# Expert layers without a barrier between them: weight pieces loaded as their rooms come free, small inputs loaded once

## The chip, the cores and the metric

One core of one Trainium2 chip. The time is device microseconds of one execution of the whole program on that core; a kernel's time is the median of its runs.

## What is computed

A network of four graph layers over 3125 nodes with 128 features and 100000 edges: a gated graph unit, two convolutions, a relational layer with 8 edge types, and a mixture of experts. Only the last one is touched:

```python
deg = jnp.clip(segment_sum(ones, dst), 1.0)[:, None]
h = x @ W_in + b_in                                   # 3125 x 256
for l in range(3):
    agg = segment_sum(h[src], dst) / deg
    logits = concatenate([h, agg], -1) @ router_W[l] + router_b[l]      # 8 experts
    gates = softmax of the top 2 of logits, 0 elsewhere
    weak = relu(einsum('nh,ehf->nef', agg, weak_W[l]) + weak_b[l])      # 4 experts
    sh = relu(einsum('nh,ehf->nef', agg, strong_W1[l]) + strong_b1[l])  # 4 experts, 512 wide
    strong = einsum('nef,efh->neh', sh, strong_W2[l]) + strong_b2[l]
    moe = einsum('ne,neh->nh', gates, concatenate([weak, strong], 1))
    h = h + sigmoid(h @ conf_W[l] + conf_b[l]) * moe
return h @ W_out + b_out
```

## The kernel before, in words

Edges are turned once into a dense matrix of counts (`A`, the tile `counts`), so that every segment sum is a matrix product on TensorE. The expert layer's code is `block_experts`. Its **input stage** parks the features `xn` in DRAM (`sp_inputs`), normalizes them (the norm runs over groups of tiles, in turns of VectorE and ScalarE) and makes `m_h`, 25 tiles of 128 nodes by 256. A barrier ends it. Then come **three layers**, each closed by a barrier of all engines. `dve_layer`, `act_layer`, `pe_layer` and `sp_layer` write down, engine by engine, the work of one layer; within an engine the order is that of the code, and between engines semaphores order it.

A layer goes like this.
- VectorE reduces `m_h` to its largest magnitude (L1738 over all of `m_h` in the first layer, L1740 over the seven chunk maxima that L1905 left in the others), TensorE spreads it (L2002, L2004), and VectorE makes a power-of-two scale of it; L1749 is the last step.
- ScalarE casts the scaled `m_h` to half precision in five pieces (L1921), VectorE writes the remainders (L1754); both halves feed the **edge sums** on TensorE (L2018), 100 matmuls for a chunk of up to 512 nodes.
- The weights come as ten pieces of 512 KB (four first matrices `w1`, four second matrices `w2`, two pairs of weak matrices `ww`) in the order of `ORDER`. Piece k is loaded as f32 into room k + 1 and split into two halves of f16 in room k, by ScalarE (L1928) and VectorE (L1772) in turn; the tenth piece is loaded into a spare part of `x_nodes`. Four pieces are split before the first chunk, the others inside it.
- Then seven chunks: the mean of the edge sums with the inverse degrees `m_invd` (L1783), the router (L2042), hidden products (L2057), strong products (L2076), weak products (L2093), and VectorE adds each expert to `m_h` (L1865, L1881). The last chunk has 309 nodes. In it the hidden blocks of expert e come in two halves, the second one after the strong products of expert e - 1.

The loads of a layer are issued from two queues. SyncE's: the ten pieces (L1720, L1724), then `m_invd` for each chunk (L1731), each of the latter after the mean of the chunk before. ScalarE's, at the very start of `act_layer` and so ahead of the casts in its program: the router's weights and biases (`m_rw`, `m_rb`, L1912 to L1915), the strong experts' hidden biases `m_b` (L1916, 2048 single elements) and the output biases `m_bias` (L1917, L1918, each repeated over 128 partitions).

Of the kernel before, what the change touches and what calls it, by code (L numbers as in the profile page):

```python
# [25 lines left out]
P = 128  # L26
# [23 lines left out]
def build_program(nc, x, src, dst, et, g_w, g_ih, g_hh, g_bih, g_bhh, c_w0, c_b0, c_w1, c_b1,  # L50
# [1503 lines left out]
    mrw_in, mb1_in, mbb_in, inv_in = sem("mrw_in"), sem("mb1_in"), sem("mbb_in"), sem("inv_in")  # L1554
# [10 lines left out]
    def block_experts(part):  # L1565
        SL = 2 * BANK
        NPC = 2 * NSG + NWK // 2
        NSH = 6
        NPR = NWK * H // BANK
        with ExitStack() as c:  # L1570
            h2 = sbuf(c, "m_h", [P, NT, H], F32)
            bcast = sbuf(c, "m_bias", [P, NE * H], F32)
            agg = sbuf(c, "m_agg", [P, KB, BANK], F32)
            agg16 = sbuf(c, "m_agg16", [P, 2, KB, BANK], F16)
            hT = sbuf(c, "m_hT", [P, KB, BANK], F32)
            rw = sbuf(c, "m_rw", [P, 2 * KB, NE + 1], F32)
            rb = sbuf(c, "m_rb", [P, NE + 1], F32)
# [6 lines left out]
            wmax, wsc, winv, wwork = (sbuf(c, f"m_wmax{i}", [P, NM], F32) for i in range(4))  # L1584

            with ExitStack() as c0:
# [6 lines left out]
                def pool_inputs():  # L1593
                    pool.iota(prio[:], pattern=[[-1, NE]], base=NE, channel_multiplier=0,
                              allow_small_or_imprecise_dtypes=True).then_inc(prio_made, 1)

                def sp_inputs():
                    sp.dma_start(xpark, xn[:].rearrange("p i f -> p (i f)")).then_inc(parked, 16)
                    sp.wait_ge(parked, 16)
# [62 lines left out]
            with ExitStack() as c0:  # L1662
                h16 = sbuf(c0, "m_h16", [P, 2, NT, H], F16)
                wroom = sbuf(c0, "m_weights", [P, NPC, SL], F32)
                b1 = sbuf(c0, "m_b1", [P, NSG * FB], F32)
# [47 lines left out]

                def sp_layer(l):
                    for k, (n_, e) in enumerate(ORDER):
                        room = loaded_piece(k)
                        if n_ == "ww":
                            r3 = room.rearrange("p (k f) -> p k f", k=KB)
                            for x_ in range(2):
                                sp.dma_start(r3[:, :, x_ * H:(x_ + 1) * H],  # L1720
                                             m_ww[l, 2 * e + x_].rearrange("(k p) h -> p k h", p=P)).then_inc(piece_in[k], 16)
                        else:
                            w_, nb = (m_w1, KB) if n_ == "w1" else (m_w2, FB)
                            sp.dma_start(room.rearrange("p (k f) -> p k f", k=nb),  # L1724
                                         w_[l, e].rearrange("(k p) f -> p k f", p=P)).then_inc(piece_in[k], 16)
                    for ci in range(NCH):
                        n = l * NCH + ci
                        c_, cw = CH[ci]
                        if n:
                            sp.wait_ge(e_mean, KB * n)  # L1730
                        sp.dma_start(invd[:, 0:cw], bass.AP(invd_row.tensor, c_, [[0, P], [1, cw]])).then_inc(inv_in, 16)  # L1731

                def dve_layer(l):
                    w_inv = {n_: scale_of(l, n_, winv) for n_ in ("w1", "w2", "ww")}
                    if l == 0:
                        vec.memset(rw[:, KB:2 * KB, NE:NE + 1], 0.0).then_inc(steps.handle, steps.up())
                        mark["rw_cleared"] = steps.n
# [17 lines left out]
                    vec.wait_ge(mb1_in, 16 * (l + 1))  # L1755
# [8 lines left out]
                    vec.tensor_scalar(b1s[:], b1[:], ks[:, 1:2], None, ALU.mult).then_inc(steps.handle, steps.up())  # L1764
# [23 lines left out]
                    def route(ci):  # L1788
# [3 lines left out]
                        vec.wait_ge(mrw_in, 64 * (l + 1))  # L1792
# [3 lines left out]
                                          rb[0:R_, None, :].to_broadcast([R_, n_, NE + 1]), ALU.add).then_inc(e_logits, 1)  # L1796
# [112 lines left out]
                def act_layer(l):  # L1909
                    if l == 0:  # L1910
                        act.wait_ge(steps.handle, mark["rw_cleared"])
                    act.dma_start(rw[:, :, 0:NE], m_rw[l].rearrange("(k p) e -> p k e", p=P)).then_inc(mrw_in, 16)  # L1912
                    act.dma_start(rw[:, 0:KB, NE:NE + 1], m_cw[l].rearrange("(k p) e -> p k e", p=P), allow_slow_non_contiguous=True).then_inc(mrw_in, 16)
                    act.dma_start(rb[:, 0:NE], bass.AP(m_rb.tensor, m_rb.offset + l * NE, [[0, P], [1, NE]])).then_inc(mrw_in, 16)
                    act.dma_start(rb[:, NE:NE + 1], bass.AP(m_cb.tensor, m_cb.offset + l, [[0, P], [1, 1]])).then_inc(mrw_in, 16)  # L1915
                    act.dma_start(b1[:], m_b1[l].rearrange("e (k p) -> p (e k)", p=P), allow_slow_non_contiguous=True).then_inc(mb1_in, 16)  # L1916
                    act.dma_start(bcast[:, 0:NWK * H], bass.AP(m_wb.tensor, m_wb.offset + l * NWK * H, [[0, P], [1, NWK * H]])).then_inc(mbb_in, 16)  # L1917
                    act.dma_start(bcast[:, NWK * H:NE * H], bass.AP(m_b2.tensor, m_b2.offset + l * NSG * H, [[0, P], [1, NSG * H]])).then_inc(mbb_in, 16)  # L1918
# [80 lines left out]
                def pe_layer(l):  # L1999
# [33 lines left out]
                    def route(ci):  # L2033
# [3 lines left out]
                        pe.wait_ge(mrw_in, 64 * (l + 1))  # L2037
                        for i, k in tiles_of(CH[ci]):
                            r_ = rows_of(i)
                            for kk in range(2 * KB):  # L2040
                                lhs = (hT if kk < KB else agg)[:, kk % KB, k * P:k * P + r_]
                                m = pe.matmul(bank[2][0:r_, k * (NE + 1):(k + 1) * (NE + 1)], lhs, rw[:, kk, :],  # L2042
# [802 lines left out]
```

## Time and profile before

| | us |
|---|---|
| median of 3 runs | 3355.61 (3353.94 to 3356.59) |
| profiled execution, its own time | 3354.32 |
| span of the profile | 3352.3 |
| TensorE matmul busy in the span | 2990.9 (89%) |
| VectorE busy | 2184.1 (65%) |
| ScalarE busy | 897.6 (27%) |

The profiled execution takes 2.0 us more than its span; the sum of the prediction is made against its time. The three expert layers are the last 1,590 us of the span but for some 33 us of output. A row of a timeline below gives: start, duration, engine, line, operation, out<-in, count, and in brackets the idle time before with what ended it. A row with SPq or ACTq is a DMA issue on the queue of SyncE or ScalarE, and its duration is the time that the issue took there, not the transfer.

### The profile page before, as it was taken

What the parts mean: (1) busy time and instruction counts of PE and PEld (TensorE: products, weight loads), DVE (VectorE), ACT (ScalarE), POOL (GpSimd) and SP (SyncE); (2) the same over time, 40 slices, a digit from 0 to 9 for tenths busy, and PEclk for the clock granted to TensorE, in tenths of its full rate; (3) what the DMA queues carried; (4) which work ended last, traced back from release to release, by engine and by line L of the source; (5) the groups of instructions that cost most, each with busy time, mean ns of one, the idle gap of its engine ahead of it and who ended that gap; (6) DMA issues with size and microseconds to landing.
All of it is one profiled execution on the core that took longest, in us unless ns stands there. A gap on an engine that the chain in (4) does not pass through costs nothing. (4 is left out here: it accounts for less than half of the span.)

```text
span 3352.3 us, 47544 instructions
## 1 busy us (share of the span) xinstructions
PE 2990.9 (89%) x18761; PEld 1803.0 (54%) x18761; DVE 2184.1 (65%) x3982; ACT 897.6 (27%) x1667; POOL 16.6 (0%) x22
## 2 busy tenths in 40 slices
PE   3777889999797999999959999988999998999997
PEld 2555555555343444444535655664656564566565
DVE  7999555554426667666666666675666675666666
ACT  3887322121212000000023222323222233222222
POOL 1000000000000000000000000000000000000000
PEclk8898999999898999999979999998999998999999
DMA  4544456563003555554330000002000002000001
GB/s 103 155 140 145 134 184 205 189 209 125 21 1 116 172 154 171 171 155 130 88 104 4 6 3 4 3 3 80 3 4 4 5 1 82 3 4 3 4 3 40
DMA packets 310670, 262.56 MB, mean 78 GB/s; under 512 B 32735, under 2 KB 289377, under 8 KB 308142
## 3 DMA queue, kind: packets, MB, share of 16 engines
q1 hardware_dynamic: 295406, 252.86, 24.7%
q10 hardware_dynamic: 14624, 5.76, 0.7%
q8 instruction: 153, 2.51, 0.3%
q0 software_dynamic: 416, 0.85, 0.1%
q14 instruction: 71, 0.58, 0.1%
HBM read 171.03 MB, written 88.41 MB: 77 GB/s over the span
## 5 line engine op out<-in xcount | busy, mean ns | idle before, releaser
L1437 PE MATMUL psum<-r_wd,r_h 128*128 128x512 fp8e4 (+1 forms) x2600 | 567.9, 374 | 13.3 <-ACT r_h L226 12.7
L2057 PE MATMUL psum<-m_agg,m_weights 128*128 128x512 f16 (+2 forms) x2016 | 423.1, 362 | 34.2 <-ACT m_agg L1964 34.2
L2018 PE MATMUL psum<-counts,m_h 128*128 128x512 fp8e4 (+2 forms) x2100 | 416.0, 354 | 29.0 <-DVE m_h L1754 29.0
L2076 PE MATMUL psum<-m_weights,x_nodes 128*128 128x256 f16 (+1 forms) x3600 | 413.0, 273 | 17.6 <-DVE m_wtmp L1862 15.9
L1437 PEld LDWEIGHTS psum<-r_wd,r_h 128*128 128x128 f16 x2600 | 240.0, 96 | 306.1 <-issue 16.8
L2076 PEld LDWEIGHTS psum<-m_weights,x_nodes 128*128 128x128 f16 (+1 forms) x3600 | 350.3, 98 | 75.1 <-DVE m_wtmp L1862 22.6
L2057 PEld LDWEIGHTS psum<-m_agg,m_weights 128*128 128x128 f16 x2016 | 197.3, 101 | 243.1 <-issue 50.1
L2018 PEld LDWEIGHTS psum<-counts,m_h 128*128 128x128 f16 x2100 | 206.2, 98 | 225.3 <-issue 35.5
L1976 ACT ACTIVATE m_hT<-m_hT,m_g 128x256 f32<-128x256 f32 x300 | 135.4, 500 | 599.5 <-DVE m_hT L1876 599.5
L1964 ACT ACTIVATE m_agg<-psum,x_nodes 128x512 f32<-128x512 f32 (+2 forms) x336 | 236.4, 717 | 145.6 <-PE psum L2057 116.2
L627 PE MATMUL psum<-oh_c,oh_s 128*128 128x150 f16 x1566 | 159.4, 244 | 84.2 <-ACT counts L653 63.5
L1862 DVE SCALAR_TENSOR_TENSOR m_wtmp<-psum,x_nodes,m_bias 128x256 f32<-128x256 f32 (+1 forms) x300 | 144.9, 483 | 120.3 <-PE psum L2076 116.8
L1876 DVE SCALAR_TENSOR_TENSOR m_hT<-psum,x_nodes,m_bias 128x512 f32<-128x512 f32 (+1 forms) x150 | 111.9, 750 | 169.7 <-PE psum L2093 169.7
L1853 DVE TENSOR_TENSOR x_nodes<-m_agg,x_nodes 128x512 f16<-128x512 f32 (+2 forms) x336 | 209.7, 624 | 11.6
L2093 PE MATMUL psum<-m_weights,m_agg 128*128 128x512 f16 x900 | 206.5, 379 | 0.0
L810 DVE TENSOR_TENSOR sym_blocks<-sym_blocks,psum 128x1024 uint16<-128x1024 uint16 (+1 forms) x169 | 110.3, 664 | 115.7 <-PE psum L791 115.3
L1452 ACT ACTIVATE r_ags<-psum 128x512 f32<-128x512 f32 (+1 forms) x52 | 26.9, 569 | 581.3 <-PE psum L1437 581.3
L627 PEld LDWEIGHTS psum<-oh_c,oh_s 128*128 128x128 f16 x1566 | 114.3, 102 | 126.7 <-issue 94.0
L652 ACT ACTIVATE strip<-psum 128x600 uint16<-128x600 f32 x239 | 162.0, 678 | 35.9 <-PE psum L627 32.9
L922 PE MATMUL psum<-counts,g_h 128*128 128x512 fp8e4 (+2 forms) x700 | 156.8, 358 | 8.0 <-PEq L104 5.0
L922 PE MATMUL psum<-counts,g_h16b 128*128 128x512 fp8e4 (+2 forms) x700 | 151.0, 352 | 5.5 <-DVE g_h16b L1074 5.5
L1865 DVE SCALAR_TENSOR_TENSOR m_h<-m_wtmp,m_g,m_h 128x256 f32<-128x256 f32 (+1 forms) x300 | 145.3, 484 | 10.7
(284 smaller groups left out, 3363.6 us busy)
## 6 DMA issues: line engine op xcount, KB each, us to landing
r_wd<-packed_sym SPq DMA_DIRECT2D x120, 640.0 KB, 4.2
packed_counts<-strip SPq DMA_DIRECT2D x21, 1800.0 KB, 7.7
sym_blocks<-packed_counts SPq DMA_DIRECT2D x88, 384.0 KB, 4.5
packed_sym<-sym_blocks SPq DMA_DIRECT2D x84, 384.0 KB, 3.3
w_stage<-in_L_gnn_strong_W SPq DMA_DIRECT2D x12, 1024.0 KB, 6.4
m_weights<-in_L_gnn_strong_W SPq DMA_DIRECT2D x21, 512.0 KB, 9.3
w_stage<-in_L_gnn_weak_W SPq DMA_DIRECT2D x3, 1024.0 KB, 6.1
m_weights<-in_L_gnn_weak_W SPq DMA_DIRECT2D x12, 256.0 KB, 9.7
```

The costliest lines, as they stand in the source:

```text
L627: m = pe.matmul(psum[:, unit_at(u, w):unit_at(u, w) + UC], oh_s[q][:, k, :, v], oh_c[q][:, k, :, v], start=True, stop=True)
L652: act.activation(typed_home, typed, ACT.Copy, scale=0.5).then_inc(kept_a, 1)
L922: m = pe.matmul(bank[bk][:, 0:cw], h16[l % 2][:, part, i, :], A[:, i, c_:c_ + cw], start=(i == 0 and part == 0), stop=(i == NT - 1 and par ...
L1437: m = pe.matmul(bank[pair[b]][:, 0:2 * cw], h16[:, part, p0 + i, :], f_[:, 2 * b:2 * b + 2, :], start=(p0 + i == 0 and part == 0), stop=(p ...
L1853: vec.tensor_tensor(s_[:, BANK:BANK + cw], wide32, s_[:, 0:cw], ALU.subtract).then_inc(s_split, 1)
L1862: vec.scalar_tensor_tensor(tmp[k % 2][0:r_, :], bank[6 + k % 2][0:r_, 0:H], k_strong[0:r_], bcast[0:r_, ge * H:(ge + 1) * H], ALU.mult, AL ...
L1865: vec.scalar_tensor_tensor(h2[0:r_, i, :], tmp[k % 2][0:r_, :], gates[ci % 2][0:r_, k, ge:ge + 1], h2[0:r_, i, :], ALU.mult, ALU.add).then ...
L1964: act.activation(agg[:, hh % 2, 0:cw], bank[4 + hh % 2][:, 0:cw], ACT.Relu, bias=b1s[:, e * FB + f:e * FB + f + 1], scale=k_hidden).then_i ...
L2018: m = pe.matmul(bank[kb][:, 0:cw], h16[:, part, i, kb * P:(kb + 1) * P], A[:, i, c_:c_ + cw], start=(i == 0 and part == 0), stop=(i == NT ...
L2057: m = pe.matmul(bank[4 + hh % 2][:, 0:cw], w_[:, i, kb, f * P:(f + 1) * P], agg16[:, j, kb, 0:cw], start=(x_ == 0), stop=(x_ == len(todo) ...
L2076: m = pe.matmul(bank[b_][0:r_, 0:H], s_[:, pa[0] * BANK + k * P:pa[0] * BANK + k * P + r_], w_[:, pa[1], f, :], start=(f == 0 and pa == PA ...
L2093: m = pe.matmul(bank[2 + pr % 2][0:r_, :], agg16[:, pa[0], kb, k * P:k * P + r_], w_[:, pa[1], kb, :], start=(y_ == 0), stop=(y_ == len(to ...
```

## The change

- The barrier at the end of each layer goes; one stays behind the last layer.
- `sp_layer` waits, from the second layer on, before it loads piece k, until the layer before has finished with the room that piece k goes into (`room_used`).
- The small inputs `m_rw`, `m_rb` and `m_b` get room for all three layers and are loaded once, in the input stage, by SyncE. The output biases `m_bias` keep one room; SyncE loads them in the input stage for the first layer, and for a later one after the last strong expert of the layer before was added.
- ScalarE issues no DMA in the layers. The clearing of a column of `m_rw` goes from VectorE to GpSimd.

```diff
@@ block_experts @@
-            rw = sbuf(c, "m_rw", [P, 2 * KB, NE + 1], F32)
-            rb = sbuf(c, "m_rb", [P, NE + 1], F32)
+            b1 = sbuf(c, "m_b1", [P, NLAY, NSG * FB], F32)
+            rw = sbuf(c, "m_rw", [P, NLAY, 2 * KB, NE + 1], F32)
+            rb = sbuf(c, "m_rb", [P, NLAY, NE + 1], F32)
...
+            def load_biases(l):
+                sp.dma_start(bcast[:, 0:NWK * H], bass.AP(m_wb.tensor, m_wb.offset + l * NWK * H, [[0, P], [1, NWK * H]])).then_inc(mbb_in, 16)
+                sp.dma_start(bcast[:, NWK * H:NE * H], bass.AP(m_b2.tensor, m_b2.offset + l * NSG * H, [[0, P], [1, NSG * H]])).then_inc(mbb_in, 16)
...
                 def sp_inputs():
                     sp.dma_start(xpark, xn[:].rearrange("p i f -> p (i f)")).then_inc(parked, 16)
+                    sp.wait_ge(prio_made, 2)
+                    for l in range(NLAY):
+                        sp.dma_start(rw[:, l, :, 0:NE], m_rw[l].rearrange("(k p) e -> p k e", p=P)).then_inc(mrw_in, 16)
+                        sp.dma_start(rw[:, l, 0:KB, NE:NE + 1], m_cw[l].rearrange("(k p) e -> p k e", p=P), allow_slow_non_contiguous=True).then_inc(mrw_in, 16)
+                        sp.dma_start(rb[:, l, 0:NE], bass.AP(m_rb.tensor, m_rb.offset + l * NE, [[0, P], [1, NE]])).then_inc(mrw_in, 16)
+                        sp.dma_start(rb[:, l, NE:NE + 1], bass.AP(m_cb.tensor, m_cb.offset + l, [[0, P], [1, 1]])).then_inc(mrw_in, 16)
+                        sp.dma_start(b1[:, l], m_b1[l].rearrange("e (k p) -> p (e k)", p=P), allow_slow_non_contiguous=True).then_inc(mrw_in, 16)
+                    load_biases(0)
                     sp.wait_ge(parked, 16)
...
+                def room_used(l, k):
+
+                    if k + 1 == NPC:
+                        sp.wait_ge(s_mixed, NSG * NT * (l + 1))
+                        return
+                    n_, e = ORDER[k + 1]
+                    if n_ == "w1":
+                        sp.wait_ge(s_hidden, hidden_at(l, NCH - 1, e, FB - 1) + 1)
+                    elif n_ == "w2":
+                        sp.wait_ge(s_mixed, mixed_at(l, NCH - 1, e, len(tiles_of(CH[NCH - 1])) - 1) + 1)
+                    else:
+                        sp.wait_ge(k_mixed, NPR * NT * (l + 1))
+
                 def sp_layer(l):
                     for k, (n_, e) in enumerate(ORDER):
                         room = loaded_piece(k)
+                        if l:
+                            room_used(l - 1, k)
...
+                    if l:
+                        sp.wait_ge(s_added, NSG * NT * l)
+                        load_biases(l)
                     for ci in range(NCH):
...
                 def act_layer(l):
-                    if l == 0:
-                        act.wait_ge(steps.handle, mark["rw_cleared"])
-                    act.dma_start(rw[:, :, 0:NE], m_rw[l].rearrange("(k p) e -> p k e", p=P)).then_inc(mrw_in, 16)
...
-                    act.dma_start(bcast[:, NWK * H:NE * H], bass.AP(m_b2.tensor, m_b2.offset + l * NSG * H, [[0, P], [1, NSG * H]])).then_inc(mbb_in, 16)
                     act.wait_ge(steps.handle, mark["h_scale", l])
...
                     pe_layer(l)
                     sp_layer(l)
-                    barrier()
+                barrier()
```

How the issues move. First ScalarE before the change, at the start of the second layer: the last six reliefs of the layer before, then the seven issues, the five casts, and the first splits.

```order
L1964 ACTIVATE m_agg<-psum,x_nodes 128x309 x6
L1912 DMA m_rw<-in_L_gnn_router_W 128x4x8
L1913 DMA m_rw<-in_L_gnn_conf_W 128x2x1
L1914 DMA m_rb<-in_L_gnn_router_b 128x8
L1915 DMA m_rb<-in_L_gnn_conf_b 128x1
L1916 DMA m_b_127<-in_L_gnn_strong_b 128x16x1
L1917 DMA m_bias<-in_L_gnn_weak_b 128x1024
L1918 DMA m_bias<-in_L_gnn_strong_b 128x1024
L1921 ACTIVATE m_h_125<-m_h,m_sc 128x1280 x5
L1928 ACTIVATE m_weights<-m_weights,m_wmax_114 128x1024 x4
```

All seven DMA rows are gone from ScalarE after the change, in each layer. They stand on SyncE instead, which after the change reads so from the input stage to the first weights (the first five small loads come three times, once for each layer):

```order
L1605 DMA x_parked<-x_nodes 128x3200
L1608 DMA m_rw<-in_L_gnn_router_W 128x4x8
L1609 DMA m_rw<-in_L_gnn_conf_W 128x2x1
L1610 DMA m_rb<-in_L_gnn_router_b 128x8
L1611 DMA m_rb<-in_L_gnn_conf_b 128x1
L1612 DMA m_b_103<-in_L_gnn_strong_b 128x16x1
...
L1589 DMA m_bias<-in_L_gnn_weak_b 128x1024
L1590 DMA m_bias<-in_L_gnn_strong_b 128x1024
L1753 DMA m_weights<-in_L_gnn_strong_W 128x2x512 x2
```

Before, the weights followed directly on the parking store and the barrier. And SyncE after the change at the start of the second layer:

```order
L1763 DMA m_invd<-invd_row 128x309
L1753 DMA m_weights<-in_L_gnn_strong_W 128x2x512 x2
L1753 DMA m_weights<-in_L_gnn_strong_W 128x4x256 x2
L1753 DMA m_weights<-in_L_gnn_strong_W 128x2x512
L1749 DMA m_weights<-in_L_gnn_weak_W 128x2x256 x4
L1753 DMA m_weights<-in_L_gnn_strong_W 128x4x256
L1753 DMA m_weights<-in_L_gnn_strong_W 128x2x512
L1753 DMA x_nodes<-in_L_gnn_strong_W 128x4x256
L1589 DMA m_bias<-in_L_gnn_weak_b 128x1024
L1590 DMA m_bias<-in_L_gnn_strong_b 128x1024
L1763 DMA m_invd<-invd_row 128x512 x2
```

The order of the pieces is that of before; the two bias loads have come between them and the first `m_invd` of the layer.

## Rows read from the trace of the kernel before

**Rows 1.** Timeline, end of the first expert layer and start of the second: TensorE, VectorE.
```profile
2232.46 1.74 PE L2057 MATMUL psum<-m_agg,m_weights 128*128 128x309 f16 x12
...
2254.91 3.24 PE L2076 MATMUL psum<-m_weights,x_nodes 128*128 128x256 f16 x27 [0.25 <-DVE x_nodes L1853]
...
2258.77 0.47 DVE L1865 SCALAR_TENSOR_TENSOR m_h<-m_wtmp,m_g,m_h 53x256 f32<-53x256 f32 x1
2259.28 0.95 DVE L1905 TENSOR_REDUCE m_hmax<-m_h 128x1 f32<-128x768 f32 x1
...
2260.62 0.16 DVE L1740 TENSOR_REDUCE m_sc<-m_hmax 128x1 f32<-128x7 f32 x1 [0.39 <-PEq L104]
...
2262.71 0.15 DVE L1749 TENSOR_SCALAR m_sc<-m_sc 128x1 f32<-128x1 f32 x1
```

**Rows 2.** Timeline, start of the second layer: ScalarE's issues and what follows.
```profile
2260.58 0.45 ACTq L1912 DMA_DIRECT2D m_rw<-in_L_gnn_router_W  x1
...
2263.70 6.24 ACTq L1917 DMA_DIRECT2D m_bias<-in_L_gnn_weak_b  x1
...
2269.97 0.48 ACTq L1918 DMA_DIRECT2D m_bias<-in_L_gnn_strong_b  x1
2270.49 6.37 ACT L1921 ACTIVATE m_h<-m_h,m_sc 128x1280 f16<-128x1280 f32 x5 [16.64 <-issue]
...
2271.96 7.40 DVE L1754 SCALAR_TENSOR_TENSOR m_h<-m_h,m_sc,m_h 128x1280 f16<-128x1280 f32 x5 [9.10 <-ACT m_h L1921]
...
2273.66 23.04 PE L2018 MATMUL psum<-counts,m_h 128*128 128x512 fp8e4 x100 [11.80 <-DVE m_h L1754]
```

**Rows 3.** Timeline, same stretch: first and fourth split, first mean.
```profile
2276.77 1.13 ACT L1928 ACTIVATE m_weights<-m_weights,m_wmax 128x1024 f16<-128x1024 f32 x1
...
2288.61 1.28 DVE L1772 SCALAR_TENSOR_TENSOR m_weights<-m_weights,m_wmax 128x1024 f16<-128x1024 f32 x1 [1.28 <-ACT m_weights L1928]
2289.81 0.74 DVE L1783 SCALAR_TENSOR_TENSOR m_agg<-psum,m_sc,m_invd 128x512 f32<-128x512 f32 x1
```

**Rows 4.** Timeline, starts of the first layer (1738) and of the third (2791).
```profile
1738.30 0.15 DVE L1749 TENSOR_SCALAR m_sc<-m_sc 128x1 f32<-128x1 f32 x1
...
1739.95 6.37 ACT L1921 ACTIVATE m_h<-m_h,m_sc 128x1280 f16<-128x1280 f32 x5 [15.01 <-issue]
...
2791.67 0.15 DVE L1749 TENSOR_SCALAR m_sc<-m_sc 128x1 f32<-128x1 f32 x1
...
2799.18 6.37 ACT L1921 ACTIVATE m_h<-m_h,m_sc 128x1280 f16<-128x1280 f32 x5 [16.36 <-issue]
```

**Rows 5.** DMA issues from 2255 to 2300: count, KB each, median us to landing.
```profile
m_weights<-in_L_gnn_strong_W SPq DMA_DIRECT2D x7, 512.0 KB, 9.3
...
m_bias<-in_L_gnn_weak_b ACTq DMA_DIRECT2D x1, 512.0 KB, 15.0
...
m_invd<-invd_row SPq DMA_DIRECT2D x2, 256.0 KB, 7.3
...
m_b<-in_L_gnn_strong_b ACTq DMA_DIRECT2D x1, 8.0 KB, 14.0
```

**Rows 6.** Windows: length, busy PE, PEld, DVE, ACT, POOL, granted clock, DMA share, GB/s.
```profile
2262.00:2266.00 4.00, 0.00 (x0) 0.00 (x0) 0.72 (x6) 0.00 (x0) 0.00 (x0) 0.58 0.91 260
2274.00:2277.00 3.00, 3.00 (x10) 1.18 (x9) 3.00 (x3) 3.00 (x4) 0.00 (x0) 0.62 1.19 331
2277.00:2280.00 3.00, 3.00 (x16) 1.36 (x14) 2.90 (x6) 0.91 (x1) 0.00 (x0) 1.00 1.03 402
```

**Rows 7.** Timeline, start of the input stage, and SyncE's first weight load behind its barrier.
```profile
1683.61 0.33 SPq L1598 DMA_DIRECT2D x_parked<-x_nodes  x1
...
1685.83 1.29 ACTq L1605 DMA_DIRECT2D m_bin<-in_L_gnn_b_in  x1
...
1687.16 1.15 ACT L218 ACTIVATE ln_sq<-m_hn 128x512 f32<-128x512 f32 x2 [6.78 <-DVE m_hn L189]
...
1728.82 2.79 SPq L1724 DMA_DIRECT2D m_weights<-in_L_gnn_strong_W  x5
```

More of the change, by code:

```diff
@@ L1553, in build_program @@
     e_high, e_low = sem("e_high"), sem("e_low")
-    mrw_in, mb1_in, mbb_in, inv_in = sem("mrw_in"), sem("mb1_in"), sem("mbb_in"), sem("inv_in")
+    mrw_in, mbb_in, inv_in = sem("mrw_in"), sem("mbb_in"), sem("inv_in")
     piece_in = [sem(f"piece_in{k}") for k in range(2 * NSG + NWK // 2)]
@@ L1568, in block_experts @@
         NSH = 6
+        MRW_IN = 80 * NLAY
         NPR = NWK * H // BANK
@@ L1664, in block_experts @@
                 wroom = sbuf(c0, "m_weights", [P, NPC, SL], F32)
-                b1 = sbuf(c0, "m_b1", [P, NSG * FB], F32)
                 xroom = xn[:].rearrange("p i f -> p (i f)")
@@ L1754, in dve_layer @@
                         vec.scalar_tensor_tensor(h16[:, 1, s, :], h2[:, s, :], sc[:, 1:2], h16[:, 0, s, :], ALU.mult, ALU.subtract).then_inc(e_low, 1)
-                    vec.wait_ge(mb1_in, 16 * (l + 1))
+                    vec.wait_ge(mrw_in, MRW_IN)
                     vec.tensor_scalar(ks[:, 0:1], sc[:, 0:1], float(H), wmax[:, l:l + 1], ALU.mult, ALU.mult).then_inc(steps.handle, steps.up())
@@ L1763, in dve_layer @@
                     vec.tensor_tensor(k_weak, sc[:, 2:3], w_inv["ww"], ALU.mult).then_inc(steps.handle, steps.up())
-                    vec.tensor_scalar(b1s[:], b1[:], ks[:, 1:2], None, ALU.mult).then_inc(steps.handle, steps.up())
+                    vec.tensor_scalar(b1s[:], b1[:, l], ks[:, 1:2], None, ALU.mult).then_inc(steps.handle, steps.up())
                     settle()
@@ L1791, in route @@
                         vec.wait_ge(prio_made, 1)
-                        vec.wait_ge(mrw_in, 64 * (l + 1))
+                        vec.wait_ge(mrw_in, MRW_IN)
                         vec.wait_ge(e_routed, n + 1)
@@ L2036, in route @@
                         pe.wait_ge(h_kept, KB * (n + 1))
-                        pe.wait_ge(mrw_in, 64 * (l + 1))
+                        pe.wait_ge(mrw_in, MRW_IN)
                         for i, k in tiles_of(CH[ci]):
@@ L2041, in route @@
                                 lhs = (hT if kk < KB else agg)[:, kk % KB, k * P:k * P + r_]
-                                m = pe.matmul(bank[2][0:r_, k * (NE + 1):(k + 1) * (NE + 1)], lhs, rw[:, kk, :],
+                                m = pe.matmul(bank[2][0:r_, k * (NE + 1):(k + 1) * (NE + 1)], lhs, rw[:, l, kk, :],
                                               start=(kk == 0), stop=(kk == 2 * KB - 1))
```

10 lines of the change are left out of this document (2 added, 8 removed).

## The prediction

> **What bounds the kernel now.** Read the busy shares first: TensorE is busy for most of the span, so a microsecond is won only where TensorE stands still or waits. The change touches one stage, the three expert layers, and there the merged timeline around the start of a layer shows one such place. The reader should follow it in this order.
>
> At the end of the first expert layer the last strong matmuls end at 2258.15 (2254.91 + 3.24), VectorE adds the last expert to `m_h` until 2259.24, reduces the maximum until 2260.23, and after the barrier starts the next layer's maximum at 2260.62; the scale of `m_h` is ready when L1749 ends, at 2262.86 [rows 1]. ScalarE should now cast `m_h` to half precision. It does so only at 2270.49, since its own queue stands before the cast: seven DMA issues from 2260.58 to 2270.45, of which the issue of the weak bias alone holds it for 6.24 us [rows 2]. VectorE's low halves follow at 2271.96 and TensorE's edge sums at 2273.66. From there TensorE works without a gap for 23.04 us, until 2296.70 [rows 2]. So the path is: scale, cast, low half, edge sums; the DMA issues of ScalarE lie on it, while the weights do not: their first split is at 2276.77, behind the casts, and the four splits that come first are done at 2289.89, well before the sums end [rows 3]. The third layer's start looks the same (scale ready at 2791.82, cast at 2799.18), and in the first layer a long reduction over all of `m_h` hides most of it (scale ready at 1738.45, cast at 1739.95) [rows 4].
>
> **The change, part by part.**
>
> *The seven issues leave ScalarE.* The handover from a ScalarE cast to VectorE takes 0.20 us: VectorE starts 1.47 us after the first cast started, and one of the five casts is 6.37 / 5 = 1.27 us [rows 2]. I take the same 0.20 for the way back. The cast can then start at 2263.06 instead of 2270.49: 7.43 us. Third layer: 2799.18 - 2792.02 = 7.16 us. First layer: 1739.95 - 1738.65 = 1.30 us [rows 4]. Together 15.89 us. A stall that goes must not meet the next late thing: VectorE is idle there (its next work is the low halves), and TensorE waits for VectorE alone.
>
> *The barrier between layers goes (two of three are on the way; the one after the last layer stays).* From the end of the maximum (2260.23) to L1740 (2260.62) are 0.39 us; a wait of VectorE on its own step is 0.04 (2259.24 to 2259.28) [rows 1]. Gain 0.35 each, 0.70 for both. Bounds: nothing, or the whole 0.39 each.
>
> *The weights are loaded as rooms come free.* This takes nothing off the path, since they were not on it [rows 3], but the path now comes 7.8 us earlier and they must keep ahead of it. Piece 0 goes into the room of expert 1's first matrix, last read by the hidden matmuls that end at 2234.20 [rows 1]; at the median landing of 9.3 us [rows 5] it is there at 2243.5, and its split is wanted at 2276.77 - 7.8 = 2269.0. The last two pieces wait for the last strong matmul (2258.15) and are split only after the first chunk's router. I cost it at 0. The cover is large: even if every piece were loaded only after 2258.15, piece 0 would be there at 2267.5. Contention of these loads with the end of a layer: in the kernel before, the edge sums run beside full DMA engines for 3.00 us (share 1.03) with 16 matmuls counted [rows 6]; their mean once the clock is up, (23.04 - 2.6) / 94 = 0.22 us, is 14 per 3 us. The full engines slow nothing there, so 0 as well.
>
> *The queue of SyncE.* Behind the waits for rooms now stand the two bias loads and the layer's first `m_invd`. The last wait ends at 2259.24; if the biases' issues cost what they cost ScalarE (6.24 + 0.48) [rows 2] the `m_invd` issue starts at 2266.0 and lands, at the 7.3 us of the crowded queue [rows 5], at 2273.3. VectorE wants it for L1783, now at 2289.81 [rows 3] and then at 2282.0. Slack 8.7 us, cost 0. The biases are wanted later still, behind the first chunk's router.
>
> *The small inputs move into the input stage.* SyncE issues 15 small loads and two biases there, after the parking store (1683.61), and has nothing else until the barrier, behind which its first weight load starts at 1728.82 [rows 7]. Price by rows 2: one layer's set holds a queue from 2260.58 until the weak bias is accepted at 2269.94, 9.4 us; three are 28 us, so SyncE is done near 1684.5 + 28 + 1 = 1713.5, 15 us before anyone waits. There is one place without cover: ScalarE's own issue of `m_bin` (1.29 us) ends at 1687.12 and its first square of the norm starts at 1687.16 [rows 7]; SyncE's first small loads now fall beside it. Whatever that issue grows by, the norm chain grows by. Lower end 0; upper end 6.24, the longest an issue was held in this trace beside a busy other queue [rows 2]. I take 0.5, near the lower end, because the set's long member (2048 single elements per layer) comes fifth, about 2 us behind the first, when `m_bin` is through.
>
> Here a rule speaks about the first term. The Trainium skill, "DMA: Bandwidth & Descriptors", section "Issuing engines are not separate DMA queues", says that issuing from several engines saves only the sequencer's issue time, which is usually small beside the transfer. If each of the seven issues were as short as the short ones (about 0.5 us, 3.5 in all), ScalarE would have been free at 2264.1 and the move would save only 1.0 us in the second layer. The row of 6.24 us decides against "usually small" here, and the sum goes by the row.
>
> **Clock.** TensorE's granted clock falls from 2.4 to 1.2 GHz in the gap: 0.58 over 2262 to 2266 puts the fall at 2262.6, and 0.62 over 2274 to 2277 puts the rise at 2276.3, 2.6 us after the matmuls begin; that slow start costs 1.3 us [rows 6]. The new start of the sums, 2273.66 - 7.78 = 2265.88, is still 3.3 us after the fall, so I expect the slow start to stay. When it ends may shift by its own size: 1.3 us either way, at each of three layers, 3.9 at most.
>
> **Sum.** 15.89 + 0.70 - 0.5 = 16.1 us off the profiled execution's 3354.32 gives 3338.2. The median of the runs is 3355.61, 1.3 above that execution, so the forecast is 3339.5. TensorE carries the shift to the end, since nothing behind the edge sums depends on a clock time.
>
> **The rivals.**
> 1. *The clock does not fall.* The gap shrinks from 15.5 to 7.7 us. If the fall fails to come in both later layers, 2 x 1.3 more is won: 3336.9. Against it: it came 4.5 us after the last strong matmul. 6%.
> 2. *ScalarE's issue of `m_bin` is held as the weak bias was.* The whole upper end is paid once: 3339.5 + 5.7 = 3345.2. For it: 6.24 us has happened on that engine. Against: what stood before that one was a 2048-element load on its own queue. 5%.
> 3. *The small loads hold the input stage's barrier.* If a set must land before the next is accepted (the weak bias landed 15.0 us after 2263.70 [rows 2, 5], 18.1 after its set began), three sets take 54.3 us and SyncE arrives at 1738.8, 10.0 late: 3349.5, within 0.2%. 5%. The same mechanism ends slower than before by over 0.2% (6.7 us) if SyncE arrives later than 1728.82 + 16.1 + 6.7 = 1751.6, thus at more than 22.4 us a set, which no row shows; at 25 us a set it would give 3339.5 + 30.7 = 3370.2. 4%. A rule stands with this one: the same page, section "Rules for kernel authors", says that a load with a non-contiguous last dimension becomes one descriptor per element. By that rule each `m_b1` load is 2048 descriptors of 4 bytes, and the trace agrees that it is slow, 14.0 us to land for 8 KB [rows 5].
> 4. *The change does not do what it says:* the rooms come free too late and all weights still load at the boundary. By the slack above the time is then the forecast's. It has no price and no chance of its own.
>
> **How the numbers follow.** The forecast holds 80%, the rivals 6, 5, 5 and 4. Low end: no input-stage cost (3339.0) and the clock's 3.9: 3335. High end: rival 2 at 3345.2, rounded up to 3346; outside are rival 3's two cases and some of the forecast's own error. A measurement of this kernel tells 0.2%, 6.7 us, from no change. Faster by more than that means below 3348.9: forecast and rivals 1 and 2, 91%, less 1 for the unforeseen, 0.90. Within 0.2%: 0.06. Slower: 0.04.
>
> **What would show it.** In the profile after: ScalarE's cast within 0.3 us of the end of the scale in all three layers; no ScalarE DMA issues there; the edge sums starting some 7.8 us earlier relative to the end of the previous layer; weight loads spread over the last 25 us of a layer; first splits directly behind the casts. In the input stage: ScalarE's first square at or shortly after 3.6 us from the stage's start, and the stage no longer than 45.2 us. It would be wrong if the first square slips, if VectorE waits for `m_invd` at the mean (L1783 before the change), or if ScalarE's splits wait for a DMA.

## The result, and the profile after

| | before | after |
|---|---|---|
| median, us | 3353.94 (5 runs, 3346.57 to 3356.59) | 3335.62 (5 runs, 3332.88 to 3337.89) |
| ratio of the changed kernel to the one before | | 0.9943, 95% interval 0.9930 to 0.9956 |
| profiled execution: time, span | 3354.32, 3352.3 | 3332.88, 3330.5 |

By the ratio the change is 19.1 us faster (14.8 to 23.5). The forecast was 16.1 us off 3355.61 and a time of 3339.5; the measured median lies just inside the low end of its range, 3335.0, and two of the five runs lie below it. Of the 3.9 us between forecast and median, 1.7 are the kernel before itself: over its five runs here its median is 3353.94, where the forecast started from 3355.61.

The merged timeline of the changed kernel at the start of the second layer answers to [rows 1, 2, 3]:

```profile
2254.78 0.95 DVE L1935 TENSOR_REDUCE m_hmax<-m_h 128x1 f32<-128x768 f32 x1
...
2255.76 0.16 DVE L1770 TENSOR_REDUCE m_sc<-m_hmax 128x1 f32<-128x7 f32 x1
...
2257.85 0.15 DVE L1779 TENSOR_SCALAR m_sc<-m_sc 128x1 f32<-128x1 f32 x1
2258.04 6.37 ACT L1942 ACTIVATE m_h<-m_h,m_sc 128x1280 f16<-128x1280 f32 x5 [8.69 <-DVE m_sc L1779]
2259.51 7.40 DVE L1784 SCALAR_TENSOR_TENSOR m_h<-m_h,m_sc,m_h 128x1280 f16<-128x1280 f32 x5 [1.50 <-ACT m_h L1942]
...
2261.20 23.66 PE L2039 MATMUL psum<-counts,m_h 128*128 128x512 fp8e4 x100 [4.21 <-DVE m_h L1784]
...
2264.32 1.13 ACT L1949 ACTIVATE m_weights<-m_weights,m_wmax 128x1024 f16<-128x1024 f32 x1
...
2276.16 1.28 DVE L1802 SCALAR_TENSOR_TENSOR m_weights<-m_weights,m_wmax 128x1024 f16<-128x1024 f32 x1 [1.27 <-ACT m_weights L1949]
2277.36 0.74 DVE L1813 SCALAR_TENSOR_TENSOR m_agg<-psum,m_sc,m_invd 128x512 f32<-128x512 f32 x1
```

The reader is to see that nothing stands between the scale (ready at 2258.00) and the cast (2258.04). The cast comes 2.28 us after the start of the maximum where it came after 9.87 us before, the edge sums after 5.44 us instead of 13.04. The first split follows the casts at once, so no piece of weights is late, and the mean at 2277.36 has its `m_invd`. The starts of the first and of the third layer in the same view answer to [rows 4]:

```profile
1737.23 0.15 DVE L1779 TENSOR_SCALAR m_sc<-m_sc 128x1 f32<-128x1 f32 x1
1737.42 6.37 ACT L1942 ACTIVATE m_h<-m_h,m_sc 128x1280 f16<-128x1280 f32 x5 [13.53 <-DVE m_sc L1779]
...
1740.59 24.55 PE L2039 MATMUL psum<-counts,m_h 128*128 128x512 fp8e4 x100 [4.22 <-DVE m_h L1784]
...
2779.62 6.37 ACT L1942 ACTIVATE m_h<-m_h,m_sc 128x1280 f16<-128x1280 f32 x5 [8.68 <-DVE m_sc L1779]
...
2782.78 23.99 PE L2039 MATMUL psum<-counts,m_h 128*128 128x512 fp8e4 x100 [4.20 <-DVE m_h L1784]
```

SyncE's queue in the timeline, from the input stage on:

```profile
1683.05 0.43 SPq L1608 DMA_DIRECT2D m_rw<-in_L_gnn_router_W  x1
...
1687.16 0.46 SPq L1612 DMA_DIRECT2D m_b<-in_L_gnn_strong_b  x1
1687.66 3.98 SPq L1608 DMA_DIRECT2D m_rw<-in_L_gnn_router_W  x1
...
1697.64 1.82 SPq L1589 DMA_DIRECT2D m_bias<-in_L_gnn_weak_b  x1
1699.51 0.43 SPq L1590 DMA_DIRECT2D m_bias<-in_L_gnn_strong_b  x1
1727.77 3.08 SPq L1753 DMA_DIRECT2D m_weights<-in_L_gnn_strong_W  x5
...
2229.73 11.78 SPq L1753 DMA_DIRECT2D m_weights<-in_L_gnn_strong_W  x5
...
2254.77 0.34 SPq L1589 DMA_DIRECT2D m_bias<-in_L_gnn_weak_b  x1
```

The small loads hold SyncE for 16.9 us (1683.05 to 1699.94) and it waits 27.8 us more for the barrier; the weights of the second layer are issued from 2229.73 on, inside the last chunk of the first. ScalarE's issue of `m_bin` and its first square, in the timeline of the input stage, answer to [rows 7]:

```profile
1684.81 1.26 ACTq L1620 DMA_DIRECT2D m_bin<-in_L_gnn_b_in  x1
...
1686.12 1.15 ACT L218 ACTIVATE ln_sq<-m_hn 128x512 f32<-128x512 f32 x2 [6.67 <-DVE m_hn L189]
```

The square starts 3.45 us after the stage's start (1682.67), 3.55 before. Last the windows of the input stage and the three layers, each from the issue or the maximum that starts it (the columns are those of [rows 6]); of the kernel before, then of the changed one:

```profile
1683.61:1728.82 45.21, 18.91 (x78) 14.13 (x78) 31.49 (x82) 9.17 (x21) 0.14 (x1) 0.74 0.14 47
1728.82:2260.62 531.80, 496.72 (x3125) 309.44 (x3125) 363.19 (x784) 154.58 (x256) 0.00 (x0) 0.97 0.05 16
2260.62:2789.58 528.96, 495.49 (x3125) 309.62 (x3125) 356.39 (x782) 153.41 (x255) 0.00 (x0) 0.97 0.05 16
2789.58:3318.75 529.17, 498.65 (x3125) 310.61 (x3125) 356.33 (x782) 153.62 (x255) 0.00 (x0) 0.97 0.05 16
```

```profile
1682.67:1727.77 45.10, 18.94 (x78) 14.14 (x78) 31.47 (x82) 9.17 (x21) 0.19 (x2) 0.74 0.33 72
1727.77:2255.76 527.99, 492.67 (x3125) 307.47 (x3125) 362.62 (x782) 154.48 (x256) 0.00 (x0) 0.98 0.07 22
2255.76:2777.35 521.59, 499.36 (x3125) 310.20 (x3125) 356.27 (x783) 153.77 (x255) 0.00 (x0) 0.97 0.05 16
2777.35:3297.57 520.22, 497.84 (x3125) 309.21 (x3125) 356.26 (x782) 153.67 (x255) 0.00 (x0) 0.98 0.02 8
```

The four stretches fell from 1635.14 to 1614.90, by 20.2 us: 0.1 in the input stage, 3.8, 7.4 and 8.9 in the layers. The other 1.6 of the 21.8 us between the two spans lie where nothing was edited (0.9 ahead of the input stage, 0.6 in the output).

### The profile page after: what moved, and what is told of

Its sections match the earlier page's. It is cut to its first block and busy times, and to the rows that moved or that the text cites. A ratio compares the mean times of both kernels' runs of the same rounds, so it can differ in the third digit from the quotient of the medians.

```text
span 3330.5 us, 47520 instructions
## 1 busy us (share of the span) xinstructions
PE 2985.8 (90%) x18761; PEld 1797.3 (54%) x18761; DVE 2182.9 (66%) x3981; ACT 897.4 (27%) x1667; POOL 16.6 (0%) x23
## 5 line engine op out<-in xcount | busy, mean ns | idle before, releaser
L1895 DVE SCALAR_TENSOR_TENSOR m_h<-m_wtmp,m_g,m_h 128x256 f32<-128x256 f32 (+1 forms) x300 | 145.3, 484 | 10.7
```

Source lines behind the costliest of these rows:

```text
L1895: vec.scalar_tensor_tensor(h2[0:r_, i, :], tmp[k % 2][0:r_, :], gates[ci % 2][0:r_, k, ge:ge + 1], h2[0:r_, i, :], ALU.mult, ALU.add).then ...
```

## The experiments

A whole run tells little of a few microseconds here: in the eleven profiles of this study the unedited part ahead of the input stage took from 1679.2 us to 1690.4 us. So each run is read twice: by its median beside runs of the kernel before on the same chip, and by the stretches above in its profile. In this table "cast" and "sums" are the times from a layer's first maximum to ScalarE's cast and to TensorE's first edge matmul, in the second layer; "stage" is the sum of the four stretches.

| run | ratio to before, 95% interval | stage | cast | sums | layer 1, 2, 3 |
|---|---|---|---|---|---|
| before | | 1635.1 | 9.87 | 13.04 | 531.8, 529.0, 529.2 |
| the change | 0.9943 (0.9930 to 0.9956) | 1614.9 | 2.28 | 5.44 | 528.0, 521.6, 520.2 |
| the change again | 0.9949 (0.9933 to 0.9966) | 1615.0 | 2.27 | 5.43 | 528.0, 521.6, 520.3 |
| barrier back | 0.9941 (0.9924 to 0.9958) | 1616.8 | 2.28 | 5.44 | 528.8, 521.6, 521.3 |
| issues kept | 0.9968 (0.9956 to 0.9981) | 1624.9 | 5.23 | 8.39 | 532.1, 524.4, 523.3 |
| hidden bias once | 0.9941 (0.9925 to 0.9958) | 1620.1 | 3.93 | 7.09 | 528.7, 522.3, 523.8 |
| cast held | 0.9990 (0.9978 to 1.0003) | 1632.0 | 10.64 | 13.79 | 528.1, 529.9, 528.9 |
| kept busy | 0.9930 (0.9911 to 0.9948) | 1611.4 | 2.28 | 5.44 | 527.5, 520.4, 518.5 |
| router among | 0.9995 (0.9985 to 1.0004) | 1631.3 | 2.28 | 5.44 | 534.2, 525.4, 526.6 |
| all | 0.9967 (0.9954 to 0.9979) | 1620.0 | 2.27 | 3.51 | 531.0, 521.6, 522.3 |
| busy and fine | 0.9915 (0.9901 to 0.9929) | 1607.5 | 2.28 | 3.52 | 525.0, 518.4, 518.9 |

### Barrier back

```diff
                     sp_layer(l)
-                barrier()
+                    barrier()
```

> The change with the barrier between the expert layers put back, so that the weights again all load at the boundary; the small inputs stay loaded once and ScalarE issues nothing. Theory A (the gain is the seven issues that left ScalarE, the barrier is worth 0.35 us a boundary, the early loading nothing): the second layer's cast starts about 0.4 us later after the end of the maximum than in the changed kernel (about 2.7 instead of 2.3 us after L1740's counterpart's release), the four first splits follow the casts without a DMA wait, and the whole is 0.7 us slower than the change, some 18 us below the kernel before. Theory B (the early loading is part of the gain): ScalarE's first split waits for its piece and the edge sums or the first hidden products start later, so that 3 us or more of a boundary come back, 6 us or more in all.

Measured: 3337.09 us beside 3356.61. The timeline of this kernel at the same place, with the first weights issued only now and the first split nonetheless right behind the casts:

```profile
2260.15 2.56 SPq L1753 DMA_DIRECT2D m_weights<-in_L_gnn_strong_W  x5
2260.19 0.16 DVE L1770 TENSOR_REDUCE m_sc<-m_hmax 128x1 f32<-128x7 f32 x1 [0.39 <-PEq L104]
...
2262.47 6.37 ACT L1942 ACTIVATE m_h<-m_h,m_sc 128x1280 f16<-128x1280 f32 x5 [9.04 <-DVE m_sc L1779]
...
2268.75 1.13 ACT L1949 ACTIVATE m_weights<-m_weights,m_wmax 128x1024 f16<-128x1024 f32 x1
```

Theory B falls: the cast has its 2.28 us and no split waits. The barrier's idle time before the maximum is 0.39 us where the change has 0.03. (Its profile is 1.9 us longer over the stage, not 0.7; the medians can't tell the two kernels apart.) What the title of the change names first, the barrier and the early weights, is worth under 2 us of the 20.2 by the stage.

### Issues kept

```diff
-                    sp.wait_ge(prio_made, 2)
-                    for l in range(NLAY):
...
                 def act_layer(l):
+                    act.wait_ge(prio_made, 2)
+                    if l:
+                        act.wait_ge(s_added, NSG * NT * l)
+                    act.dma_start(rw[:, l, :, 0:NE], m_rw[l].rearrange("(k p) e -> p k e", p=P)).then_inc(mrw_in, 16)
...
+                    act.dma_start(b1[:, l], m_b1[l].rearrange("e (k p) -> p (e k)", p=P), allow_slow_non_contiguous=True).then_inc(mrw_in, 16)
+                    load_biases(l)
```

> No barrier between the layers and weights loaded as rooms come free, as in the change, but ScalarE still issues all seven small loads at the start of each layer (from the second layer on after the last strong expert was added). Theory A1 (the issue of the weak bias was held because the weights of the other queue were going through the engines beside the 2048 single elements): with the weights gone the seven issues take about 5 us, the cast starts near 5 us after the last addition instead of 11.3 us after it as before, and the kernel gains some 6 us a boundary, about 12 us in all. Theory A2 (the issue is held by the 2048 elements whatever runs beside them): the seven issues take 9 to 10 us again, the cast moves by 1.3 us only, and the kernel gains about 3 us in all.

(`load_biases` issues on ScalarE in this kernel, and SyncE's small loads in the input stage are gone.) Measured: 3345.56 us beside 3356.61, ratio 0.9968, 10.7 us, where A1 had about 12. ScalarE's issues in the timeline, start of the third layer:

```profile
2787.78 0.39 ACTq L1932 DMA_DIRECT2D m_rw<-in_L_gnn_router_W  x1
...
2789.76 0.46 ACTq L1936 DMA_DIRECT2D m_b<-in_L_gnn_strong_b  x1
2790.25 3.09 ACTq L1589 DMA_DIRECT2D m_bias<-in_L_gnn_weak_b  x1
2793.37 0.46 ACTq L1590 DMA_DIRECT2D m_bias<-in_L_gnn_strong_b  x1
```

A1 holds, with 6.1 us for the seven issues instead of its 5. The issue behind the 2048 elements is held for 3.09 us here, and was for 5.57 to 7.03 us in the kernel before, where the weights went through the engines at the same time. This kernel shows both cases by itself: in its first layer, where the weights still load beside the small ones, the same issue is held for 7.53 us. So the early loading does have a use that the prediction did not see: it halves the hold, in a kernel that still has it.

### Hidden bias once

The kernel before with this edit alone:

```diff
+            b1 = sbuf(c, "m_b1", [P, NLAY, NSG * FB], F32)
...
                 def sp_inputs():
                     sp.dma_start(xpark, xn[:].rearrange("p i f -> p (i f)")).then_inc(parked, 16)
+                    for l in range(NLAY):
+                        sp.dma_start(b1[:, l], m_b1[l].rearrange("e (k p) -> p (e k)", p=P), allow_slow_non_contiguous=True).then_inc(mb1_in, 16)
...
-                    act.dma_start(b1[:], m_b1[l].rearrange("e (k p) -> p (e k)", p=P), allow_slow_non_contiguous=True).then_inc(mb1_in, 16)
```

> The kernel before with one edit: the strong experts' hidden biases m_b of all three layers are loaded once in the input stage by SyncE; the other six loads stay with ScalarE, weights and barrier stay. Theory A1 and A2 both have the long hold behind m_b: without it six issues take about 3.5 us, ScalarE is free near the time at which the scale is ready, the cast starts about 4 us after the barrier instead of 9.9, and the kernel gains 5 to 6.5 us a boundary, 10 to 13 us in all (the first layer gains up to 1.3). Theory C (issues are held by whatever fills the queues, the weights above all): the weak bias is still held for 4 us or more and the gain is under 5 us in all.

Measured: 3336.64 us beside 3356.61. The timeline at the start of the second layer:

```profile
2265.80 0.54 ACTq L1918 DMA_DIRECT2D m_bias<-in_L_gnn_weak_b  x1
...
2266.37 0.90 ACTq L1919 DMA_DIRECT2D m_bias<-in_L_gnn_strong_b  x1
2267.32 6.37 ACT L1922 ACTIVATE m_h<-m_h,m_sc 128x1280 f16<-128x1280 f32 x5 [10.69 <-issue]
```

The weak bias is accepted in 0.54 us, with the weights beside it as before. Theory C falls: the full queues alone hold nothing, the element-wise load does. One of seven loads carried 5.9 of the 7.6 us that the cast gained in this layer (9.87 to 3.93, of 9.87 to 2.28). The size was missed: 10 to 13 us were expected, the stage gained 15.0 and the median 20.0 (14 to 25 by the interval), and the difference was not traced. By the time of a whole run this one edit can't be told from the change; by the stage it is 5.2 us behind it: 3.1 us at the two later starts, 0.7 for the two barriers, and the rest in the scatter described below.

### Cast held

```diff
                     act.wait_ge(steps.handle, mark["h_scale", l])
+                    if l:
+                        for _ in range(6):
+                            back_n["n"] += 1
+                            act.activation(h16[:, 0, H5[0], :], h2[:, H5[0], :], ACT.Copy, scale=sc[:, 1:2]).then_inc(held_back, 1)
+                            act.wait_ge(held_back, back_n["n"])
```

> The changed kernel, but in the second and third layer ScalarE casts the first five tiles six more times ahead of the real casts (about 8 us), so that the cast starts as late as before the change while all else of the change stays. Theory A (the gain is the earlier cast and nothing else): each of the two layers, from the start of one maximum to the next, is 7.5 to 8.5 us longer than in the changed kernel, near 529 us as before; the whole is 15 to 17 us slower than the change. Rival (the barrier, the early loads or something later in the layer carries part of the gain): the two layers stay 2 us or more below the 529 us of before.

Measured: 3354.11 us beside 3356.51. The timeline at the start of the second layer:

```profile
2254.62 8.33 ACT L1945 ACTIVATE m_h<-m_h,m_sc 128x1280 f16<-128x1280 f32 x6 [8.69 <-DVE m_sc L1780]
2262.99 6.37 ACT L1948 ACTIVATE m_h<-m_h,m_sc 128x1280 f16<-128x1280 f32 x5
```

The hold is 8.4 us (10.64 against 2.28), and the two layers are 8.3 and 8.6 us longer than in the change, 529.9 and 528.9. A microsecond ahead of the cast is a microsecond of the layer. Against the kernel before, whose casts came 0.8 and 1.0 us earlier than the held ones, what stays of a layer behind its cast must be compared: it is 519.3 us against 519.1 in the second layer, so that nothing else carries its gain. In the third it is 518.2 against 519.6, and 1.4 us of that layer's gain are left over without the early cast.

### Kept busy

```diff
+                    def keep_busy(n):
+                        for _ in range(n):
+                            pe.matmul(bank[0][:, 0:BANK], ones_f[:].bitcast(F16)[:, 0:P], A[:, 0, 0:BANK], start=True, stop=True)
...
+                    keep_busy(9 if l else 21)
                     pe.wait_ge(steps.handle, mark["h_max", l])
...
                     pe.matmul(bank[7][:, 0:1], ones_f[0:1, :], sc[0:1, 1:2], start=True, stop=True).then_inc(max_spread, 1)
+                    keep_busy(17)
```

> The changed kernel plus matmuls whose result nobody reads (128x512, into a bank that is free) on TensorE in the gap at the start of each expert layer: 21 or 9 before the maximum is spread and 17 after it. The theory that the slow start is the granted clock: the clock stays at 2.4 GHz until the edge sums start, the first chunk's 100 edge matmuls take 21.6 us instead of 24.6, 23.7 and 24.0, and the kernel is about 7 us faster than the change, near 3328 us. Rival: the clock does not stay up over the gap or the edge sums are paced by VectorE's low halves (1.48 us for 10 matmuls, 2.15 at full clock, so it should not): no gain, or a loss of up to 2 us where the extra matmuls delay the spreading of the maximum.

Measured: 3332.01 us beside 3356.61; by the medians it can't be told from the change, by the stage it is 3.5 us faster, half of the expected 7. TensorE in the timeline, start of the second layer, and one window of the same stretch:

```profile
2257.79 2.12 PE L2025 MATMUL psum<-counts,ones_f 128*128 128x512 fp8e4 x9
...
2261.14 3.84 PE L2025 MATMUL psum<-counts,ones_f 128*128 128x512 fp8e4 x17
2265.41 21.74 PE L2048 MATMUL psum<-counts,m_h 128*128 128x512 fp8e4 x100 [0.43 <-DVE m_h L1784]
```

```profile
2262.00:2265.00 3.00, 2.98 (x14) 1.16 (x12) 1.47 (x3) 2.75 (x3) 0.00 (x0) 1.00 1.04 350
```

Where TensorE worked on through the gap, the granted clock stays at 1.00 and the 100 edge matmuls take 21.74 us instead of 23.66; in the change the granted clock fell in the gap. The windows of the change (columns as in [rows 6]) show the fall and the late rise:

```profile
2256.00:2259.00 3.00, 0.63 (x3) 0.35 (x3) 1.11 (x7) 0.96 (x1) 0.00 (x0) 0.88 0.98 345
2262.00:2265.00 3.00, 3.00 (x9) 1.07 (x8) 3.00 (x3) 3.00 (x3) 0.00 (x0) 0.50 0.08 30
2265.00:2268.00 3.00, 3.00 (x15) 1.42 (x14) 2.82 (x9) 0.45 (x1) 0.00 (x0) 0.98 0.00 0
```

The clock falls at about 2258.3, 4.7 us after the last strong matmul, and is at its lower level, 1.2 GHz, until about 2265.1, 3.9 us into the sums, against 2.6 us in [rows 6]. The Trainium skill, "TensorE: Matmul & The Clock Gate", section "Part 1: The HAM clock gate", puts it this way round: the slow level is the default and activity lifts it. The trace agrees: the clock is low in the idle stretch and comes back only with the edge sums under way. Over the three layers the sums gain 7.0 us (24.55, 23.66 and 23.99 to 21.75, 21.74 and 21.74), but the stage only 3.5: half of it is given back, 2.3 of 3.5 us in the first layer. There the clock fell as the 17 unread matmuls began; they took 5.51 us and held the sums until 4.2 us after the cast instead of 3.2. And behind the sums the clock was at its lower level for 6.8 us more than in the change, from the router's matmuls of the first chunk on and again from the third's. In the two later layers 0.7 and 0.5 us are given back, and the place was not settled.

### Router among, and all

```diff
-                        route(ci)
+                        early = [range(4 * j, 4 * j + 4) for j in range(len(ts) - 1)] if more else []
+                        route(ci, (lambda k: edges(ci + 1, [0], early[k])) if more else None)
                         hidden(ci, 0, range(FB))
                         if more:
-                            edges(ci + 1, range(KB - 1))
+                            edges(ci + 1, [0], range(4 * len(early), NT))
```

> The changed kernel with one new order on TensorE: in each chunk but a layer's last, eight edge matmuls of the next chunk stand behind the router's matmuls of each tile but the last, instead of all after the hidden products. Theory D (the differences that the cast does not explain are the granted clock, which falls at the router's matmuls of 9 columns and stays low for about 7 us of full work behind them): the clock no longer falls there, each of 18 chunks gains up to 3 us, and the kernel gains 20 to 50 us on the change. Rival E (the clock falls all the same, or VectorE's router and gates, now some 5 us later in the chunk, become what the strong products wait for): between no gain and a loss of 3 us a chunk.

> The changed kernel with the unread matmuls in the gaps, the order of the run before, and the casts cut finer (pieces of 1, 1, 2, 3, 4, 5, 5 and 4 tiles in place of five of 5), so that the edge sums start after one tile. If theory D holds: what the run before gains, plus some 3.5 us for the gaps, plus 1.5 us a layer for the finer start, 28 us or more below the change. If rival E holds: about 8 us below the change less what the new order loses.

Measured: 3354.61 us and 3346.28 us beside 3356.51: the new order costs 16 us of stage alone (1631.3 against 1614.9) and 12.5 us in company (1620.0 against the 1607.5 of the last run, which is the same but for it and a number of unread matmuls). Rival E holds; the change's gain over the kernel before is all but gone. Two groups of the waits over the layers, first in the kernel with the new order alone, then in the change (us in total, times, longest):

```profile
ACT x_nodes L1975 <- DVE x_nodes L1852: 230.3, 18, 14.8
...
DVE x_nodes L1825 <- PE psum L2063: 85.0, 18, 6.5
```

```profile
ACT x_nodes L1975 <- DVE x_nodes L1852: 180.0, 18, 11.1
...
DVE x_nodes L1825 <- PE psum L2063: 21.9, 18, 2.6
```

The router's result comes later, VectorE's gates with it, and ScalarE's exponential (L1975) stands in its queue before the hidden products' relu. TensorE then waits for both, as its timeline in the first chunk of the kernel with the new order alone shows:

```profile
1786.85 4.15 PE L2081 MATMUL psum<-m_agg,m_weights 128*128 128x512 f16 x12 [2.76 <-ACT m_agg L1985]
...
1812.88 4.46 PE L2100 MATMUL psum<-m_weights,x_nodes 128*128 128x256 f16 x24 [4.68 <-DVE m_wtmp L1892]
```

The router matmuls shown by the same timeline ran at full clock (0.51 and 0.59 us for four), and over the three layers the clock was at its lower level for 55 us instead of 72, so the clock half of theory D held in part. But TensorE had no matmul for 108 us instead of 80, and that wait cost more.

### The change again, and busy and fine

> The changed kernel once more, beside the others, to see how far one execution of it differs from the next. The parts before the expert layers, which no edit touches, should differ by up to some us (1682.7 to 1689.4 us in the profiles so far), the starts of the layers not at all (cast 2.28 us after the maximum), and the rest of a layer by 1 to 2 us.

Measured: 3337.47 us beside 3356.51. The part ahead of the input stage was 1685.1 us against 1682.7, while the stage repeats to 0.1 us, better than the 1 to 2 us a layer expected. The last run is the best version found, the change with the unread matmuls and finer casts:

```diff
-                H5 = [slice(i, i + 5) for i in range(0, NT, 5)]
+                H5_AT = [0, 1, 2, 4, 7, 11, 16, 21, NT]
+                H5 = [slice(a_, b_) for a_, b_ in zip(H5_AT, H5_AT[1:])]
...
+                    keep_busy(9 if l else 30)
...
+                    keep_busy(9)
```

> The changed kernel with unread matmuls in the gaps (30 ahead of the first layer's maximum, 9 ahead of the others', 9 behind each) and the casts cut into pieces of 1, 1, 2, 3, 4, 5, 5 and 4 tiles; the order of the router is the change's own. From the two runs that hold these parts: the edge sums start 3.51 us after the maximum instead of 5.44, and their 100 matmuls take about 22 us instead of 23.7 to 24.6. If TensorE is the bound right behind them, each layer is 3 to 4 us shorter than in the change (about 518 us for the second and third), and the kernel 9 to 12 us faster, near 3326 us. Rival: the sums are then paced by VectorE's finer low halves and the clock falls at another place behind the router, so that 3 us or less are left in all.

Measured: 3328.87 us beside 3356.96, ratio 0.9915 (0.9901 to 0.9929), faster than both kernels. Its timeline at the start of the second layer, 3.52 us behind the maximum:

```profile
2262.20 1.02 PE L2049 MATMUL psum<-counts,m_h 128*128 128x512 fp8e4 x4 [0.23 <-DVE m_h L1785]
2263.41 21.12 PE L2049 MATMUL psum<-counts,m_h 128*128 128x512 fp8e4 x96 [0.19 <-ACT m_h L1943]
```

The layers are 3.0, 3.2 and 1.3 us shorter than in the change, 7.4 us in all of the 9 to 12 expected. In the first one 30 unread matmuls were too many: they held the spreading of the maximum, and the cast came 10.3 us behind the layer's start instead of 9.6.

## Why the prediction was right in its mechanism, and which step failed

**The seven issues leave ScalarE: right, in place and size.** The cast gained 7.59, 7.33 and 1.48 us where 7.43, 7.16 and 1.30 were forecast. The difference is the handover, taken as 0.20 us by analogy and 0.04 in the timeline. The run with the cast held shows that this is all that counts in the second layer and all but 1.4 us in the third. But the step named the wrong unit. Not seven issues cost 9.9 us; six cost 3.9 and the hold behind one element-wise load the rest. The prediction had the row of 6.24 us in hand and took it as the weak bias's own price, though its rival 2 names the load that stood before it. Against the Trainium skill, "DMA: Bandwidth & Descriptors", section "Issuing engines are not separate DMA queues", it sided with the row, which was right; the skill's "usually small" is true of the six.

**The barrier: right.** 0.39 us became 0.03; 0.35 each had been taken.

**Early weights at no gain: right**, by the run with the barrier back. Pieces land in a median of 3.9 us in their new place (9.3 in [rows 5]), and the contention that was costed at nothing does not show: TensorE's last stretch of the first layer, from the same hidden matmuls to the last strong one, takes 25.68 us beside these loads, 25.68 with the barrier back and took 25.69 before.

**SyncE's queue: right with room to spare.** The two biases were issued in 0.8 us, not 6.7, and the `m_invd` issue followed at 2255.63.

**The small inputs in the input stage: 0.5 us was charged, nothing was paid** (45.21 to 45.10). Rival 2 and both cases of rival 3 fall: the three sets and the two biases hold the queue for 16.9 us, where 29 were taken, because each set was priced at the 9.4 us that ScalarE's had cost beside the weights. (The 6.24 us that bounds rival 2 is not the longest hold in the trace before: in the first layer the same issue took 7.03.)

**The clock: right that it falls, and its bound was used.** The slow start grew by 0.8, 0.6 and 0.8 us, within the 1.3 allowed. Rival 1 fell: the clock went down 4.7 us after the last strong matmul, as it had after 4.5 before.

**The rest of a layer: this is the step that failed.** The sum put everything behind the edge sums at nothing, "TensorE carries the shift to the end, since nothing behind the edge sums depends on a clock time". The terms, as measured, come to 16.4 + 0.7 + 0.1 = 17.2 us. The stage gained 20.2, the median 19.1 by the ratio. Of the 3.0 us between, the slow starts took 2.2 away, so that 5.2 came from the rest of the layers: about 2.8 in the first and 2.4 in the third, none in the second. That the low end held is luck: its 3.9 us stood for slow starts that grow shorter, and they grew longer.

What stays of a layer behind its cast is not a constant: 518.3 to 520.7 us in the first, 518.0 to 520.1 in the third, over the change, the kernel before and the runs with barrier back, issues kept and hidden bias once. Within one kernel it repeats (the change again, to 0.1 us), between kernels it moves by up to 2 us. The granted clock sorts these times. It falls at the router's matmuls of some chunks: in the first layer before, at the first and the second chunk's (four of them take 1.00 us at 1856.67 instead of 0.59), in the change only at the first's. Adding up its shortfall over windows of 2 us, behind the first 28 us of a layer, gives the time at the lower level:

| | kernels | behind the cast, us | at the lower level, us |
|---|---|---|---|
| first layer | the change, the change again, cast held | 518.3 to 518.4 | under 4 |
| first layer | before, barrier back, issues kept, hidden bias once | 519.0 to 520.7 | 13.6 to 20.6 |
| third layer | the change, the change again, issues kept, cast held | 518.0 to 518.2 | 17.0 to 17.2 |
| third layer | before, barrier back, hidden bias once | 519.0 to 520.1 | 20.5 |

In the second layer, which moves by 0.9 us only, there is no such order. So the clock at the later routers goes with the 5.2 us; that it is their cause was not shown, since no run changed it alone, and why it fell less often in the change stays open. The forecast let the clock move in the slow start only; 2 us more a layer behind it, and the scatter of the unedited parts, belonged into the low end.

## What to carry to other kernels

When an engine starts late behind its own DMA issues, look at which issue is long and then at the one before it: here a load of single elements delayed what came next on its queue, not itself. Move or reshape that load first, and weigh a larger restructuring by what is left after that. And where layers are compared by a few microseconds, cut the profile into stretches at the same events; stretches that no edit touches moved more here than the whole gain of some edits.

## What was not expected of the hardware

- The issue behind the 2048 single elements of `m_b` took 5.57, 6.24 and 7.03 us with 5 MB of weights moving beside it (7.53 us in the first layer with issues kept), 2.84 and 3.09 us without them, and 3.98, 1.89 and 1.82 us on SyncE's queue in the input stage. The load's own issue took 0.43 to 0.63 us in these two places, and 0.87 and 1.41 us once each in the input stage of two other runs. With the load gone and the weights still there, the same issue took 0.54 us.
- A gap of 7.6 us on TensorE between the strong matmuls and the edge sums, with only the short spreading of the maximum in it, cost 1.9 and 2.3 us in the 100 matmuls behind it (23.66 and 23.99 us in the change, 21.74 with the gap filled).
- The part of the program ahead of the input stage, the same instructions in all, took 1679.2 to 1690.4 us in eleven profiles.
